# One exp over the two score banks of a run; a tile's value products behind its first run of scores, its sums behind the second

## The reference

```python
def attention(q, k, v, kv_mask=None):
    s = jnp.einsum('bqhd,bkhd->bhqk', q, k) * SCALE
    if kv_mask is not None:
        s = jnp.where(kv_mask[:, None, None, :], s, jnp.float32(-1000000000.0))
    p = jax.nn.softmax(s, axis=-1)
    return jnp.einsum('bhqk,bkhd->bqhd', p, v)

img_x = attention(q, k_img, v_img)
txt_x = attention(q, k, v, kv_mask)
out = (txt_x + img_x).reshape(b, -1, DIM)
...
x = x + jnp.tanh(g_xattn[0]) * _L0_xattn_ref(_layernorm(x, axis=-1), ctx_2048, ...)
x = x + jnp.tanh(g_ffn[0]) * _L0_ffn_ref(_layernorm(x, axis=-1), ...)
```

## Time and profile before

| | |
|---|---|
| median of 3 runs | 3864.08 us |
| profiled execution, own time | 3863.82 us |
| its span in the trace | 3861.6 us |
| PE busy | 3348.9 us, 87% of the span |
| DVE busy | 2314.6 us, 60% |
| ACT busy | 1534.5 us, 40% |
| granted TensorE clock, mean | 0.941 |

### The profile page before, as it was taken

One profiled execution on the slowest core, in us unless ns is written; L12 is line 12 of the kernel. 1 busy time (PEld: TensorE's weight loads), 2 busy tenths in 40 slices (PEclk: granted clock), 3 DMA queues, 4 the chain that ended last, 5 costly groups with the idle time before them and its releaser, 6 DMA issues. The chain is left out here.

```text
span 3861.6 us, 55479 instructions
## 1 busy us (share of the span) xinstructions
PE 3348.9 (87%) x18048; PEld 1824.0 (47%) x18048; DVE 2314.6 (60%) x3780; ACT 1534.5 (40%) x2933; POOL 15.7 (0%) x34
## 2 busy tenths in 40 slices
PE   6999999967999999999999999999985651799993
PEld 5877777753333333333333333333324430677772
DVE  5766666646466666666666666666635658433335
ACT  3444334322455555555555555555551110122222
POOL 0000000000000000000000000000000000000000
PEclk8999999987899999999999999999997775899997
DMA  5666666685435253443525344452404542101004
GB/s 147 164 166 168 164 166 167 167 119 122 103 69 112 61 115 72 100 93 80 110 63 115 72 101 91 82 111 62 104 6 136 163 153 86 69 22 44 22 22 174
DMA packets 405977, 402.04 MB, mean 104 GB/s; under 512 B 43568, under 2 KB 326256, under 8 KB 403320
## 3 DMA queue, kind: packets, MB, share of 16 engines
q1 hardware_dynamic: 363272, 367.44, 40.4%
q10 hardware_dynamic: 42624, 33.56, 2.6%
HBM read 262.98 MB, written 137.92 MB: 104 GB/s over the span
## 5 line engine op out<-in xcount | busy, mean ns | idle before, releaser
L834 ACT ACTIVATE at_probs<-at_st 128x512 f32<-128x512 f32 (+1 forms) x1664 | 913.8, 595 | 940.0 <-PE at_st L713 932.4
L862 DVE TENSOR_REDUCE at_cm<-at_mx 128x2 f32<-128x896 f32 x768 | 822.2, 1090 | 555.9 <-PE at_mx L729 555.9
L713 PE MATMUL at_st<-at_qst,at_kst 101*128 101x512 f32 (+1 forms) x1664 | 705.1, 470 | 73.9 <-ACT at_probs L834 50.7
L713 PEld LDWEIGHTS at_st<-at_qst,at_kst 101*128 101x128 f32 (+1 forms) x1664 | 271.3, 184 | 679.5 <-issue 344.1
L764 PE MATMUL at_acc<-at_probs,at_ones 128*32 128x512 f32 (+2 forms) x3584 | 471.7, 601 | 22.0 <-ACT at_ev L814 22.0
L752 PE MATMUL at_acc<-at_probs,at_vt 128*32 128x512 f32 (+2 forms) x3584 | 478.7, 608 | 0.9 <-ACT at_probs L834 0.9
L729 PE MATMUL at_mx<-at_kmx,at_qmx 33*128 33x448 f32 (+1 forms) x2048 | 386.0, 429 | 43.3 <-DMA at_kmx<-stack_rows 33.4
L729 PEld LDWEIGHTS at_mx<-at_kmx,at_qmx 33*128 33x128 f32 x2048 | 185.7, 188 | 263.6 <-issue 230.0
L862 DVE TENSOR_REDUCE at_top<-at_mx 128x2 f32<-128x514 f32 x256 | 176.9, 691 | 137.5 <-PE at_mx L729 137.5
L1274 ACT ACTIVATE ff_h<-ff_psa,ff_b1c,alpha 128x512 f32<-128x512 f32 x128 | 99.6, 779 | 378.3 <-PE ff_psa L1256 378.3
L764 PEld LDWEIGHTS at_acc<-at_probs,at_ones 128*32 128x32 f32 (+2 forms) x3584 | 107.0, 110 | 300.1 <-issue 237.0
(11 more groups left out here) (182 smaller groups left out, 4030.6 us busy)
## 6 DMA issues: line engine op xcount, KB each, us to landing
at_kst<-k_high SPq DMA_DIRECT2D x256, 200.1 KB
at_kmx<-k_high SPq DMA_DIRECT2D x64, 400.2 KB
at_kst<-k_low SPq DMA_DIRECT2D x128, 200.1 KB
pj_xin<-in_ctx_dram SPq DMA_DIRECT2D x96, 256.0 KB, 4.2
k_high<-pj_kh SPq DMA_DIRECT2D x96, 256.0 KB, 3.1
k_low<-pj_kl SPq DMA_DIRECT2D x96, 256.0 KB, 4.7
values<-pj_vs SPq DMA_DIRECT2D x96, 256.0 KB, 4.5
at_vt<-values SPq DMA_DIRECT2D x32, 768.0 KB
```

The costliest lines, as they stand in the source:

```text
L713: pe.matmul(st[0:kn, h % 2, :], kst[p][:, h, t * P:t * P + kn], qst[p][:, h, :], start=True, stop=True).then_inc(S["st_done"], 1)
L834: act.activation(probs[0:kn, SLOT[t], h, :], st[0:kn, h % 2, :], ACT.Exp, scale=SCALE).then_inc(S["exp_done"], 1)
L862: dve.tensor_reduce(dst, mx[:, 2 * slot:2 * slot + 2, 0:kn], AX.X, ALU.max).then_inc(S["mx_free"], 1)
```

## The change

ACT applies exp once per run, to both banks (1024 columns), and raises `exp_done` by two. It waits until both scores of the run are made. The copies and evacuations stand behind the exp of the same run: those that stood between the two exps of a run now stand behind the pair. On PE `sums` of tile t - 1 moves from the first run of tile t (behind `values`) to its second run, behind the scores and the maxima there.

```diff
--- before.py
+++ after.py
@@ -787,6 +787,7 @@
                                     sums(G - 1, q)
                         elif t > 0 and run == 0:
                             values(G, i, par, t - 1)
+                        elif t > 0:
                             sums(G, t - 1)
 
             pe.wait_ge(S["const_set"], NC)
@@ -826,22 +827,21 @@
                 last = isinstance(G, int) and G == GROUPS - 1
                 for t in range(KT):
                     kn = keys(t)
-                    for h in range(HG):
-                        n = NST * G + HG * t + h
-                        act.wait_ge(S["st_done"], n + 1)
-                        if h == 0:
+                    for run in range(2):
+                        act.wait_ge(S["st_done"], NST * G + HG * t + 2 * run + 2)
+                        if run == 0:
                             ring(G, t)
-                        act.activation(probs[0:kn, SLOT[t], h, :], st[0:kn, h % 2, :], ACT.Exp, scale=SCALE).then_inc(S["exp_done"], 1)
-                        if not last and h % 2 and (t, h // 2) in top_at:
-                            copy_top(G + 1, 1 - par, top_at[t, h // 2])
+                        act.activation(probs[0:kn, SLOT[t], 2 * run:2 * run + 2, :], st[0:kn, :, :], ACT.Exp, scale=SCALE).then_inc(S["exp_done"], 2)
+                        if not last and (t, run) in top_at:
+                            copy_top(G + 1, 1 - par, top_at[t, run])
                         if not known(G, 1):
-                            if (t, h) == (0, 3):
+                            if (t, run) == (0, 1):
                                 evacuate(G - 1, 1 - par, VI, 0, "v_done", "v_free")
-                            if (t, h) == (1, 0):
+                            if (t, run) == (1, 0):
                                 evacuate(G - 1, 1 - par, SI, 1, "s_done", "s_free")
-                        if (t, h) == (11, 2):
+                        if (t, run) == (11, 1):
                             evacuate(G, par, VT, 0, "v_done", "v_free")
-                        if (t, h) == (12, 0):
+                        if (t, run) == (12, 0):
                             evacuate(G, par, ST, 1, "s_done", "s_free")
 
             act.wait_ge(S["const_set"], NC)
```

## The result

The changed kernel takes 3739.69 us (median of 4 runs, 3716.81 to 3755.09) against 3865.2 before: ratio 0.9671, 95% interval 0.9626 to 0.9716. Six further runs on another occasion gave 3735.42 and the same ratio (0.9635 to 0.9707). The forecast was 3720. The profiled execution took 3734.04, its span 3731.9.

What follows compares the result with a forecast made beforehand. PE was taken to bound attention, partly waiting for the second run's exps. Tile gains 2.4 + 0.5 + 0.1 + 1.1 + 0.3 = 4.4 per group, 32 groups, 142 us: 3863.8 - 142 = 3722, said as 3720, range 3675 to 3785.

Steps and rivals of the forecast that it cites:

- What bounds it, and the wait's place: Attention on PE: all slack in a tile's first run, all waiting for the second run's two exps, about 0.12 + 0.25 per tile.
- The chain: Each run of a tile: scores, exp of both, next scores; 0.77 + 1.02 + 0.05 = 1.84 us, upper end 2.11.
- PE's work: PE's matmuls in each run: values before scores 0.98, sums 0.97; moving the sums costs 0.1 more per tile.
- Tiles 2 to 9: Steady tiles of a group: runs of 2.23 and 2.02, so 4.25 for 4.55; gain 2.4 per group.
- Tile 10: Near a group's end: 2.19 plus a second run set by the chain, 1.84; 4.03 for 4.55, gain 0.5.
- Tile 11: Next to last tile of a group, with the tops: 4.37 for 4.51, gain 0.1.
- Tile 12: Last tile of a group, ACT late: 2.3 plus 1.8, so 4.1 for 5.24; gain 1.1.
- Tile 0: First tile of a group: 6.33 for 6.62, gain 0.3.
- rival (c): Slower: regular PE waits of 0.2 in tiles 10 and 12 bring the clock down; up to 3943, chance 0.06.
- Rival (a): In attention's tiles the chain is dearer, 2.11; loses 1.5 per group, 48 us, total 3770; chance 0.12.
- (b): No change: the stall moves on whole, since two banks under one exp are no double buffer; about 3864, chance 0.04.
- (d): Exp over two banks does not run as one, or takes twice the time per column; 4260, chance 0.02.

Runs made afterwards that it cites:

- the group of 60.18 without a dip: A group behind the loop in the changed kernel (joint exp) with its maxima steps in 16 pairs; that kernel measured 3759.44 us, ratio 0.9716.

## Why the prediction was right, and what it missed

**What bounds it, and the wait's place.** Right, and shown by the two halves of the change run apart: the waiting was for the exps of the second run, and PE work beside them removes it. The move of the sums alone brings the group to 56.81; the joint exp alone makes it longer.

**The joint exp.** Priced at 1.02, measured 1.024. The chain was priced at 1.84 and is 1.90: exp starts 0.83 after the pair's start in the second run (1734.52 - 1733.69) and 0.91 in the first (1732.42 - 1731.51), not 0.77. It binds only in tile 10's second run and in tile 12, as said. What I did not ask is whether this half of the change was worth having. It is not: it costs 0.47 per group, 15 us. 0.25 of that is shown to be the bank, since two exps one after the other let PE have the first one back early; 0.22 is in tile 12, where the place of an evacuation changed with it. I had the numbers for the first part (exp from 0.54, bank free 0.6 later) and spent them on the pair as a whole.

**PE's work.** 0.98 for values before scores is 1.00, 0.97 for sums 1.00; both now start behind maxima, and sums that start behind values still take 0.97 (2051.94 - 2050.97 with the exp joined and the sums left in place). I had named values over 0.98 as a sign of being wrong, and by 0.02 it is met, too little to move the sum. The values behind maxima cost 0.88 before other 32-column matmuls and 1.00 before scores or maxima, so leaving this kind costs 0.12. The Trainium skill's "TensorEngine Tiling (Array Packing)", Key Properties, says that a change of tiling mode drains the array. The traces agree for the leaving of the 32-column matmuls and show no such cost for the leaving of the full array (0.33 from the second score to what follows, 0.34 from the first to the second); that the 0.12 is a drain was not tried apart. Tiles 2 to 9 were to take 4.25; the one shown takes 4.24, and all of them 4.22 to 4.33, 4.25 on the mean.

**Tiles 10 to 12 and 0.** Tile 10: 1769.64 - 1765.55 = 4.09 for 4.03, the chain's 0.06; its gain is 0.40 and not 0.5, as it took 4.49 before and I had counted it with the mean of 4.55. Tile 11: 1774.03 - 1769.64 = 4.39 for 4.37. Tile 12: 4.23 for 4.1, with a wait of 0.70 before the values that I had overlooked: the evacuation of their bank stands behind the second exp and the copy. Tile 0: 1727.28 - 1720.97 = 6.31 for 6.33.

**The sum.** 4.4 per group were said, 4.21 came: 135 us for 142. Measured are 125.5 (medians), 129.8 (profiles) and 132 (the other occasion). The rest of the miss is rival (c) in a small form. From the start of the first group to that of the last the profile before has 1917.6 us and that after 1796.8, 120.8 less where 31 x 4.21 = 130.5 would be steady. (The two profiles differ by 9 us more outside this stretch.) Before, the first three groups are 11.4 longer than steady ones, and the clock is at half for 34 us in them. After, the first group is 8.8 longer, and the 31st 12.3, by this:

```profile
2670.53 1.06 PE L752 MATMUL at_acc<-at_probs,at_vt 128*32 128x512 f32 x8
2673.42 0.73 PE L713 MATMUL at_st<-at_qst,at_kst 101*128 101x512 f32 x2 [1.82 <-ACT at_probs L834]
```

```profile
2672.34 1.02 ACT L834 ACTIVATE at_probs<-at_st 128x1024 f32<-128x1024 f32 x1 [3.28 <-issue]
```

```profile
2674.10:2698.00 23.90, 23.90 (x87) 6.75 (x86) 10.84 (x13) 7.14 (x7) 0.00 (x0) 0.50 0.00 1
```

130.5 + 11.4 - 8.8 - 12.3 = 120.8. Of the 12.3 about 1.9 are the wait itself, as the group of 60.18 without a dip shows. So (c) was right that a stall can cost its multiple through the clock, and wrong about which: with the regular short waits of tiles 10 and 12 the clock stayed at 1.00, and it fell behind one wait of 1.8. That the wait made it fall rests on three executions and has one against it (1.73, no dip); no run varied the wait alone. Rival (a) is ruled out by 1.024 and 1.90, (b) and (d) by the group of 57.28. One small slip: 4.4 of 61.49 is 7% and not 8%; the DMA share came out at 0.46, not 0.43.

**What stays open.** Why ScalarE is late once behind the loop. It is so in all five profiles with the joint exp, by 2.2 to 2.6 us, and in none of those with single exps. With the sums left in place it is this one:

```profile
3322.62 1.02 ACT L833 ACTIVATE at_probs<-at_st 128x1024 f32<-128x1024 f32 x1 [3.15 <-issue]
```

In all five the late exp starts 1.4 to 1.5 us behind an 8 KB packet on an instruction queue (at 2670.9 and 2689.5 in the two profiles of the changed kernel), so a late fetch of code is likely; it was not tried. Against it: the kernels with single exps have such packets too (at 2685.6 with the sums moved only), at the end of the 31st group, and no exp is late there. How long the clock stays low at the start of attention differs from run to run and is open as well.

## What to carry to other kernels

Ask what an engine has to do between handing a buffer over and needing it back, run by run. Here one run of a tile was 3.31 us long and the other 1.19, so that the second pair of exps had too little work beside it; the same work split evenly covered both pairs. When a change has two parts, price each alone. Here the part that merges instructions only lengthens the chain: both results must be there before ScalarE starts, and both buffers come back at its end. Merging costs where other engines wait for the merged instruction; whether it pays where the engine itself is full, no run here shows. Read how long a matmul really takes from start to start; busy time hides the waits.

## What the runs showed of the hardware that was not expected

- ScalarE's exp takes 1.024 us for 128x1024 over two banks of PSUM, 0.595 for 128x512, and two of the latter 1.08 back to back.
- A group of four side by side 32-column fp32 matmuls costs 0.88 ahead of the next such group and 1.00 ahead of scores or of 64-row maxima (0.97 ahead of scores where another such group stands before it). Two scores cost 0.66 to 0.67 whatever follows them. A first step of maxima costs 0.40, a second right behind it 0.21 (448 columns) or 0.12 (258).
- One PE wait of 1.8 to 2.1 us was followed by 23.9 us of half clock with PE busy throughout, in three executions; in a fourth with a wait of 1.7 it was not. With PE waiting 0.78 in every tile, and up to 1.17 at each group's end, attention's mean clock was 0.83; the time rose by 13%, and about two thirds of the rise go with the half clock.
